# Slot attention in a twelve-stage kernel: score buffers released by PSUM bank, one merged query and key weight, gate terms put into PSUM, reset gate first

## The reference, cut to what matters

```python
Pn = rmsnorm(P, input_norm_w)
k_proj = Pn @ Wk.T;  v_proj = Pn @ Wv.T
for _ in range(3):
    q = rmsnorm(slots, slot_norm_w) @ Wq.T
    attn = softmax(q @ k_proj.T * 256 ** -0.5, axis=slots)
    attn = attn / (attn.sum(over context) + 1e-6)
    slots = gru_cell(attn @ v_proj, slots, wi, wh, bi, bh)
# gru_cell: r = sigmoid(ir + hr); z = sigmoid(iz + hz)
#           n = tanh(inn + r * hn); return (1 - z) * n + z * h
```

## Time and profile before

| | us |
|---|---|
| median of three runs | 1587.63 |
| the profiled execution | 1585.95 |
| its span in the trace | 1583.7 |
| first round, first score to last attend (14.40 to 107.61) | 93.2 |
| tail and head between rounds one and two (107.88 to 125.70) | 17.8 |

### The profile page before, as it was taken

The page is one execution under the profiler, slowest core; times in us unless marked ns, Lnnn a source line. Parts: engine busy times, 40 slices in busy tenths (PEclk is TensorE's granted clock), DMA queues, the critical chain, the costliest instruction groups (busy, mean ns, idle before and its releaser), DMA issues. The chain is left out here.

```text
span 1583.7 us, 29660 instructions
## 1 busy us (share of the span) xinstructions
PE 1460.7 (92%) x11444; PEld 1106.4 (70%) x11444; DVE 926.7 (59%) x2822; ACT 764.3 (48%) x1787; POOL 82.0 (5%) x74
## 2 busy tenths in 40 slices
PE   7998999987999888899999999999999798889987
PEld 6977979955767654467777777777776696656765
DVE  5654545547466442377777777777777275444434
ACT  5744535523122131266676666676766681323222
POOL 2310000000000000200000000000000000000000
PEclk9999999988999999899999999999999998989999
DMA  9946414310156379511100001111100300507760
GB/s 330 325 141 238 161 48 163 117 40 8 61 225 233 131 282 344 221 36 37 37 32 21 24 35 36 37 36 37 36 2 2 124 2 1 228 1 241 271 258 4
DMA packets 66011, 182.28 MB, mean 115 GB/s; under 512 B 5201, under 2 KB 47185, under 8 KB 64465
## 3 DMA queue, kind: packets, MB, share of 16 engines
q1 hardware_dynamic: 65152, 171.98, 30.2%
q10 hardware_dynamic: 720, 8.42, 1.3%
HBM read 179.86 MB, written 0.52 MB: 114 GB/s over the span
## 5 line engine op out<-in xcount | busy, mean ns | idle before, releaser
L1978 ACT ACTIVATE cross_s<-cross_s,cross_shift 128x896 f32<-128x896 f32 x224 | 215.2, 1031 | 39.2 <-DVE cross_shift L2062 39.2
L1972 ACT COPY cross_eT<-cross_ring 128x512 f32<-128x512 f32 x280 | 153.1, 591 | 143.3 <-PE cross_ring L1900 143.3
L1900 PEld LDWEIGHTS cross_ring<-consts,cross_s 128*128 128x128 f32 x1568 | 168.3, 141 | 56.3 <-issue 44.2
L1900 PE MATMUL cross_ring<-consts,cross_s 128*128 128x128 f32 x1568 | 197.0, 277 | 6.1 <-ACT cross_s L1978 6.1
L2053 DVE CUSTOM_DVE_ANT_0 cross_s<-cross_scores,cross_mask,cross_top 128x448 f32<-128x448 f32 x224 | 141.3, 681 | 84.5 <-PE cross_scores L1892 84.5
L436 ACT ACTIVATE slots_probs<-slots_scores,slots_bias,ctx_rinv 128x128 f32<-128x128 f32 x294 | 130.0, 460 | 109.7 <-DVE slots_bias L484 109.7
L2053 DVE CUSTOM_DVE_ANT_0 cross_s<-cross_scores,cross_mask,cross_half_max 128x448 f32<-128x448 f32 x224 | 141.4, 682 | 13.4 <-PE cross_scores L1892 13.3
L155 PE MATMUL slots_scores<-slots_qkT,slots_ctxT 128*128 128x128 f32 x1176 | 139.9, 277 | 9.1 <-DMA slots_ctxT<-in_ctxT 8.3
L155 PEld LDWEIGHTS slots_scores<-slots_qkT,slots_ctxT 128*128 128x128 f32 x1176 | 138.4, 194 | 13.1 <-DMA slots_ctxT<-in_ctxT 9.3
L386 PE MATMUL slots_attended<-ctx_rows,slots_probs 128*128 128x257 f32 x588 | 135.2, 380 | 1.2 <-DVE slots_pooled L498 1.1
L1892 PE MATMUL cross_scores<-cross_keysT,cross_qz 32*128 32x448 f32 x896 | 121.8, 589 | 4.3 <-DVE cross_half_max L2053 3.1
(11 more groups left out here) (794 smaller groups left out, 2141.2 us busy)
## 6 DMA issues: line engine op xcount, KB each, us to landing
slots_ctxT<-in_ctxT SPq DMA_DIRECT2D x42, 896.0 KB, 4.7
ctx_rows<-in_ctx_rows SPq DMA_DIRECT2D x28, 896.0 KB, 7.3
ctx_rows<-in_moe_w SPq DMA_DIRECT2D x24, 1024.0 KB, 9.7
cross_ctxT<-in_ctxT SPq DMA_DIRECT2D x13, 896.0 KB, 4.5
padded_ctxT<-in_ctxT SPq DMA_DIRECT2D x12, 896.0 KB, 4.6
plain_ctxT<-in_ctxT SPq DMA_DIRECT2D x12, 896.0 KB, 4.7
local_layers<-in_w_local SPq DMA_DIRECT2D x2, 4552.0 KB, 14.5
weights_region<-in_moe_w SPq DMA_DIRECT2D x8, 1024.0 KB, 10.9
```

The lines of the kernel that those rows point to most:

```text
L1900: last = pe.transpose(bank(("turn", u, t))[:, j * P:(j + 1) * P], s_buf[:, u % 2, j, t * P:(t + 1) * P], K.ident)
L1972: act.copy(eT[:, u % 2, t], bank(item)).then_inc(st("emptied_act"), 1)
L1978: act.activation(rows, rows, ACT.Exp, bias=shift[:, u % 2, j:j + 1], scale=SCALE).then_inc(st("exp"), 1)
```

## The change

1. **By bank.** `score`, the `ctxT` loads, `maxima` and `exponentials` are each cut into a part of four tiles and one of three (`BANK_TILES`), with semaphores and loads for each.
2. **Order of the first round.** Mean squares run one group ahead, ScalarE's between the two parts of the exponentials, VectorE's behind `normalise`. The loads of rows are sent by a table, `ROWS_AT`.
3. **One weight.** Wq and Wk are multiplied once on TensorE and scaled by both norm weights (`qk_weight`). A head is then one product of two matmuls from `slotsT`, a scaling by 1/rms, two transposes and a copy. The slots themselves are transposed, so the norm runs beside.
4. **Pooling.** The division by the sum is put into the transposition: `pooled` times a diagonal matrix `diag`. The input norm weight goes into Wv once.
5. **Gates.** Biases are put into PSUM by a product with the identity, the old slots' part is accumulated on them at moments given in the code, and ScalarE reads the gates from PSUM. Reset comes first, then the candidate, then update.
6. **TensorE's idle products** go from the heads; six stand behind the last round. The loads of the next stages' weights on ScalarE's queue are sent behind the square root instead of ahead of it.

```diff
-ROWS_AHEAD = 2
 ROWS_SENT = 4
+ROWS_AT = {1: [1], 2: [2], 3: [3, 4], 4: [5, 6], **{n: [n + 2] for n in range(5, GROUPS - 2)}}
+BANK_TILES = (range(0, 4), range(4, TILE))
...
+                    for s, part in enumerate(BANK_TILES):
+                        if n >= 2:
+                            sp.wait_ge(st("scored"), 2 * (n - 2) + s + 1)
+                        keys = slice(part[0] * P, part[-1] * P + P)
+                        sp.dma_start(ctxT[:, b, :, keys], T["ctxT"][g:g + 1, :, :, keys].rearrange("o p c m -> p (o c) m")).then_inc(st(f"ctxT_in{b}{s}"), 16)
...
-                    pe.wait_ge(st(f"ctxT_in{b}"), (n // 2) * 16 + 16)
-                    if n >= 2:
-                        pe.wait_ge(st("exp"), n - 1)
-                    for t in range(TILE):
-                        last = product(pe, sc[b][:, t], [(ctxT[:, b, c, t * P:(t + 1) * P], qkT[:, c]) for c in range(DC)])
-                    last.then_inc(st("scored"), 1)
...
                 K.weights.wait(pe, "slots")
+                fold_qk(0)
                 for it in range(SLOT_ITERS):
-                    idle_products(pe, K, scores[:, 1024:1536], 10 if it else 4)
+                    pe.wait_ge(st("slots_ready"), it + 1)
...
+                    if it == 0:
+                        fold_qk(1)
+                        pe.wait_ge(st("qk_weight"), DC)
+                    pe.wait_ge(st("slotsT"), it + 1)
+                    product(pe, qk_mm, [(slotsT[:, k], qk_weight[:, k]) for k in range(DC)]).then_inc(st("qk_mm"), 1)
+                    pe.wait_ge(st("qk"), it + 1)
+                    transposes(pe, qkT_mm, qk, K.ident, DC).then_inc(st("qkT_mm"), 1)
+                    if it:
+                        reset_slots()
...
+                    if it == 0:
+                        K.weights.wait(pe, "gates")
+                        pe.wait_ge(st("gate_rows"), 1)
+                        reset_hcand_rows()
+                    else:
+                        update_rows()
+                        update_slots(0)
                     pe.wait_ge(st("pooled"), it + 1)
-                    transposes(pe, pooledT_mm, pooled, K.ident, DC).then_inc(st("pooledT_mm"), 1)
+                    for c in range(DC):
+                        last = pe.matmul(pooledT_mm[:, c], pooled[:, c * P:(c + 1) * P], diag[:, :], start=True, stop=True)
+                    last.then_inc(st("pooledT_mm"), 1)
+                    if it == 0:
+                        reset_slots()
+                    else:
+                        update_slots(1)
                     pe.wait_ge(st("pooledT"), it + 1)
                     for c in range(DC):
                         last = product(pe, updT_mm[:, c], [(wv[:, k, c * P:(c + 1) * P], pooledT[:, k]) for k in range(DC)])
                     last.then_inc(st("upd_mm"), 1)
+                    for k in range(DC):
+                        pe.matmul(hcand_mm, slotsT[:, k], wh[:, k, 2 * D:], start=False, stop=False)
+                    if it == 0:
+                        inn_rows()
                     pe.wait_ge(st("updT"), it + 1)
                     for k in range(DC):
-                        last = pe.matmul(rz, updT[:, k], wi[:, k, 0:2 * D], start=False, stop=k == DC - 1)
-                    last.then_inc(st("rz_mm"), 1)
-                    product(pe, inn, [(updT[:, k], wi[:, k, 2 * D:]) for k in range(DC)]).then_inc(st("gates_mm"), 1)
+                        last = pe.matmul(reset, updT[:, k], wi[:, k, 0:D], start=False, stop=k == DC - 1)
+                    last.then_inc(st("reset_mm"), 1)
+                    for k in range(DC):
+                        last = pe.matmul(inn, updT[:, k], wi[:, k, 2 * D:], start=False, stop=k == DC - 1)
+                    last.then_inc(st("inn_mm"), 1)
+                    if it == 0:
+                        update_rows()
+                        update_slots(0)
+                        update_slots(1)
+                    for k in range(DC):
+                        last = pe.matmul(update, updT[:, k], wi[:, k, D:2 * D], start=False, stop=k == DC - 1)
+                    last.then_inc(st("update_mm"), 1)
+                    if it + 1 < SLOT_ITERS:
+                        pe.wait_ge(st("hcand"), it + 1)
+                        reset_hcand_rows()
+                        pe.wait_ge(st("cand_in"), it + 1)
+                        inn_rows()
+                    else:
+                        idle_products(pe, K, scores[:, 1536:2048], 6)
...
+                    g, b, a = n % GROUPS, n % 2, n % HELD
+                    for s, part in enumerate(BANK_TILES):
+                        act.wait_ge(st("bias"), 2 * n + s + 1)
+                        for t in part:
+                            last = act.activation(probs[:, a, t], sc[b][:, t], ACT.Exp, bias=bias[:, a, t:t + 1],
+                                                  scale=K.rinv[:, g * TILE + t:g * TILE + t + 1], accum_out=total[:, a, t:t + 1])
+                        last.then_inc(st("exp"), 1)
+                        if s == 0 and n + 1 < GROUPS:
+                            squares(n + 1)

...
+                    act.wait_ge(st("reset_mm"), it + 1)
+                    act.activation(gate[:, 0:D], reset, ACT.Sigmoid).then_inc(st("reset"), 1)
                     act.wait_ge(st("cand_in"), it + 1)
                     act.activation(cand[:, :], cand[:, :], ACT.Tanh).then_inc(st("cand"), 1)
+                    act.wait_ge(st("update_mm"), it + 1)
+                    act.activation(gate[:, D:2 * D], update, ACT.Sigmoid).then_inc(st("update"), 1)
...
                     for g in range(GROUPS + 1 + SLOT_LAG):
                         n = it * GROUPS + g
                         if g < GROUPS:
                             maxima(n)
-                        if it == 0 and g + ROWS_AHEAD < GROUPS:
-                            squares(g + ROWS_AHEAD)
                         if 1 <= g <= GROUPS:
                             normalise(n - 1)
+                        if it == 0 and g + 1 < GROUPS:
+                            squares(g + 1)
+                        if it == 0 and g == GROUPS:
+                            K.weights.wait(dve, "gates")
+                            link(dve.tensor_tensor(W["bi"][:, D:2 * D], W["bi"][:, D:2 * D], W["bh"][:, D:2 * D], ALU.add))
+                            dve.tensor_tensor(W["bh"][:, D:2 * D], W["bi"][:, 0:D], W["bh"][:, 0:D], ALU.add)
+                            for k in range(DC):
+                                last = dve.tensor_scalar(wv[:, k], wv[:, k], W["in_w"][:, k:k + 1], None, ALU.mult)
+                            last.then_inc(st("gate_rows"), 1)
```

More of the change, by code:

```diff
@@ L315, in stage_slots @@
         at = [attended[:, b * 512:b * 512 + D + 1] for b in range(2)]
-        slotsT_mm, normedT_mm = two(attended[:, 0:D]), two(mm[:, 0:D])
-        qT_mm, qkT_mm = two(mm[:, 512:512 + D]), two(mm[:, 512 + D:1024])
+        slotsT_mm, qk_mm = two(attended[:, 0:D]), attended[:, 512:512 + D]
+        qkT_mm = two(attended[:, 0:D])
+        qk_weight_mm = [mm[:, c * 512:c * 512 + D] for c in range(DC)]
         pooledT_mm, updT_mm = two(scores[:, 0:D]), two(scores[:, 512:512 + D])
-        rz, hn, inn = mm[:, 0:512], mm[:, 512:768], mm[:, 768:1024]
+        reset_hcand, reset, hcand_mm, inn = mm[:, 0:2 * D], mm[:, 0:D], mm[:, D:2 * D], mm[:, 512:512 + D]
+        update = scores[:, 1024:1024 + D]
         def tiles(g):
@@ L387, in attend, with fold_qk, reset_hcand_rows, inn_rows @@
                     last.then_inc(st("attended"), 1)
+                def fold_qk(c):
+                    product(pe, qk_weight_mm[c], [(wq[:, k, c * P:(c + 1) * P], wk[:, k]) for k in range(DC)]).then_inc(st("qk_weight_mm"), 1)
+                def reset_hcand_rows():
+                    pe.matmul(reset_hcand, K.ident, W["bh"][:, D:3 * D], start=True, stop=False)
+                def inn_rows():
+                    pe.matmul(inn, K.ident, W["bi"][:, 2 * D:], start=True, stop=False)
+                def update_rows():
+                    pe.matmul(update, K.ident, W["bi"][:, D:2 * D], start=True, stop=False)
@@ L389, in _, with reset_slots, update_slots @@
+                def reset_slots():
+                    for k in range(DC):
+                        pe.matmul(reset, slotsT[:, k], wh[:, k, 0:D], start=False, stop=False)
+                def update_slots(k):
+                    pe.matmul(update, slotsT[:, k], wh[:, k, D:2 * D], start=False, stop=False)
                 K.weights.wait(pe, "slots")
+                fold_qk(0)
                 for it in range(SLOT_ITERS):
-                    idle_products(pe, K, scores[:, 1024:1536], 10 if it else 4)
@@ L430, in _ @@
                 norm_scalar(act, st, "ln", lnb)
-                def exponentials(n):
-                    g, b, a = n % GROUPS, n % 2, n % HELD
-                    act.wait_ge(st("bias"), n + 1)
-                    for t in range(TILE):
-                        last = act.activation(probs[:, a, t], sc[b][:, t], ACT.Exp, bias=bias[:, a, t:t + 1],
```

(12 more changed lines are left out.)

139 lines of the change are left out of this document (57 added, 82 removed).

## The result

The changed kernel takes 1572.78 us (median of five runs, 1570.65 to 1576.36) against 1587.63 for the kernel before: ratio 0.9899, 95% interval 0.9883 to 0.9915. That is 14.85 us faster, where 28 to 30 were forecast. The profiled execution is 1572.78 us with a span of 1570.5, so in the profiles the gain is 13.2.

What follows compares the result with a forecast made beforehand. TensorE was taken to bound the group loops, a serial chain the stretches between. Gains in loops, heads, tails and next stage summed to 28.4 us, giving 1557.5 from the profile, 1559.2 from the median; forecast 1558, range 1551 to 1571.

Steps and rivals of the forecast that it cites:

- no wait in round three and 0.5 us in round two: Start of the group loops: predicted waits of the third scores for `ctxT`; rounds two and three gain 3.8 and 2.85 us.
- its bounds are 0 and 3.1: Third scores of round two: limits set on the 0.5 us wait, 3.1 us being the wait before the change.
- The ring is under the 6.17 of TensorE, so after the start it catches up: Round one's loop: the dependency cycle through bias, exponentials, squares and `rinv` takes 5.7 us a group, below TensorE's 6.17.
- Halving the packets of `ctxT` I take at nothing: `ctxT` loads in the group loops: smaller packets were claimed to cost 0, with 350 GB/s when busy either way.
- the next stage: Start of the stage after the rounds: six idle products keep the clock up, 3 us gained, bounds -0.6 and 3.4.
- Later stages only shift: Everything after the next stage's start: claimed to move earlier in time without gaining or losing any.
- heads: Start of rounds two and three, slots to first score: 3.9 us instead of 6.2, each gaining 2.3 us.
- the other tails: Rounds two and three, last `add` to new slots: 8.1 us instead of 11.6, a gain of 3.5 us.
- A: Rival, round one: GpSimd's step meets the 1.09 us product, a ring turn takes 6.8 us; 8 us lost, 1566; chance 0.11.
- B: Rival: starts still wait, round two 3.1 us, round one loses the clock, next stage gains nothing; 1566; chance 0.12.
- C: Rival: TensorE's clock falls at the tails' starts and in heads; 34 us given back, 1591.5; chance 0.05.
- D: Rival: unseen limits leave half of each chain term and nothing in the loop, about 1578 to 1583; chance 0.04.

Runs made afterwards that it cites:

- Experiment 3: The kernel before, with the two loads of the next stage's weights sent behind round two's square root instead of ahead of it; 1592.78 us, ratio 1.0007.
- 4: The changed kernel, with both loads of the next stage's weights sent in round one's tail, ahead of ScalarE's wait for `reset_mm`; 1566.77 us, ratio 0.9857.
- 12: The changed kernel, with both loads of the next stage's weights sent behind the reset sigmoid of round one; 1568.52 us (one run).
- 9: The kernel before, with both weight loads sent early, ahead of the wait for round one's gates; 1586.81 us, ratio 0.9982.
- Experiment 11: The changed kernel with weight loads sent in round one's tail, each `ctxT` load from the third group on bringing only one of two chunks; 1565.32 us (one run).
- 2: The changed kernel, with each half of `ctxT` contiguous in DRAM and SBUF, in pieces of 4096 and 3072 bytes per partition; 1576.09 us, ratio 0.9907.
- 6: The changed kernel, with weight loads sent in round one's tail and contiguous `ctxT` halves in packets of 4 and 3 KB; 1565.43 us, ratio 0.9846.
- Experiment 8: The changed kernel, with weight loads sent in round one's tail and without the six idle products behind the last gate product; 1563.92 us (one run).
- experiment 10: The changed kernel, with weight loads in round one's tail, contiguous `ctxT` halves and `add(n-3)` ahead of the squares on VectorE; 1565.17 us, ratio 0.9846.

## Why the prediction was wrong, step by step

The direction was right and the time 14.8 us too low. The step that failed is "no wait in round three and 0.5 us in round two", in its second half, with "its bounds are 0 and 3.1". The wait measured 7.41 us and its slowed scores cost 1.5 more: 8.4 us beyond the forecast, of the 8.7 by which that loop missed it. I had most of the numbers for it. The DMA list gives 4100, 768 and 896 KB (the first two were not among my rows), the rows about 350 GB/s when the DMA is busy, and the send time moves against the first score from 8.0 us ahead to 3.3. The wait before was no upper bound: what hid the load was the head and its lead, and the change shortened both by 4.7 us in all. The sum 3.10 + 4.7 = 7.8 could be made from the rows, and the wait measured 7.41. Experiment 3 shows the send time alone (2.29 later, 2.68 more wait), 4 and 12 show it taken back (waits of 0.34 and 2.32), and 9 shows that the kernel before had little to gain from it.

The second step is in "The ring is under the 6.17 of TensorE, so after the start it catches up", a loop of round one in which only the start and 0.1 us at the end are held up and the DMA costs nothing. Loop 1 gained 2.1 us instead of 4.65. Its DMA share rose to 0.90 from 0.83. Its waits for `ctxT` and `add` behind attend 0 add up to 1.8 us, and from start to start they cost 2.6: the steps are 3.82 and 3.70 us long where 3.05 is normal (`ctxT`), 3.85 where 3.12 is, and the last one about 0.4 too long (`add`). That is about the miss of 2.55. Experiment 11 brings the round to its forecast by removing half of the bytes and packets of `ctxT`. "Halving the packets of `ctxT` I take at nothing" misreads the edit, since they fall to a quarter, from 7168 to 2048 and 1536 bytes; what that costs round one no run settles (experiments 2 and 6 disagree).

The third, smaller, is the next stage: 2.0 us for 3, within its bounds. Experiment 8 puts the idle products at 2.4. The sum of the terms is 28.45. With 8.7 us missed in loop 2, 2.55 in loop 1, 1.0 in the next stage, 0.4 in all other terms and the 2.7 lost later ("Later stages only shift", which these two executions do not bear out), the 13.2 us of the profiles are left.

What held: the first score at 13.09 (forecast 13.45), attend 0 at 24.23 after 1.28 us of idle time (25.0 and 1.6), heads of 3.97 us from the slots' end (3.9), 10.05 from the last `add` to slots in round one (10.0), 3.25 for 3.5 in the other tails, round three 2.74 for 2.85, and the first two rows of the next stage at 1.97 and 2.83 us (1.8 and 2.7).

The rivals: A did not occur. The biases of the first groups, on VectorE's timeline, stand 5.66 to 6.05 us apart, where 5.7 was forecast, and the product (L545) ends at 24.18, before GpSimd's step begins at 26.06, which takes 0.21:

```profile
21.88 0.20 DVE L535 SCALAR_TENSOR_TENSOR slots_bias<-slots_top,ctx_rinv 128x4 f32<-128x4 f32 x1 [2.65 <-POOL ctx_rinv L363]
...
23.09 1.09 DVE L545 TENSOR_TENSOR slots_probs<-slots_probs,slots_weight 128x896 f32<-128x896 f32 x1
...
27.93 0.19 DVE L535 SCALAR_TENSOR_TENSOR slots_bias<-slots_top,ctx_rinv 128x4 f32<-128x4 f32 x1 [1.93 <-POOL ctx_rinv L363]
...
33.59 0.19 DVE L535 SCALAR_TENSOR_TENSOR slots_bias<-slots_top,ctx_rinv 128x4 f32<-128x4 f32 x1 [1.72 <-POOL ctx_rinv L363]
```

The Trainium skill's exclusion of VectorE and GpSimd on a shared port (SBUF — State Buffer, Who interferes with whom) could not show here, since the product ended before GpSimd's step began. B came nearest, in its place, though not in its size or its parts: a start that waits, in round two alone, with a wait of 7.41 us where I gave it 3.1, while the next stage kept its gain. Even its 1566 is 7 us too low, and its part in round one's start did not occur: the third scores there did not wait and kept their pace. C did not occur in the changed kernel's tails or heads, whose records run at full clock; what clock was lost there was lost in the wait for `ctxT`. It can occur: in experiment 10 one head did lose the clock (0.51), with gaps no longer than elsewhere, and cost 1.9 us. The Trainium skill (TensorE: Matmul & The Clock Gate, A second HAM failure mode) tells of such swings from short gaps between groups of matmuls; that row agrees, and most executions here show none. D is excluded by the table, where the terms of the chain are there in full.

The fourth and sixth experiments are faster than both kernels (0.9857 and 0.9846, where the changed kernel has 0.9899); the simplest edit that pays is to send the weights when ScalarE has issued round one's exponentials. Left open: why the clock falls in some heads and starts and not in others, what the smaller packets cost round one, and whether the 2.7 us that are gone by the end recur.

## What to carry to other kernels

When a chain is shortened, look at every load that is sent during it and stands ahead of a transfer wanted after it: its hiding time shrinks by the same amount. Add up the bytes from the send to the first transfer that is waited for and divide by the rate of a full DMA; in the five traces here where the DMA stayed full, the end of the wait followed the send time, and not the work that was made faster. And do not count on slack in a stretch with a DMA share of 0.83: here round one waited for DMA as soon as its engines were faster.

## What the runs showed of the hardware

- 5.9 MB on two queues took 17.1 (the changed kernel and experiment 12), 17.6 (before) and 17.8 us (experiment 3) from the first issue to the start of the work that needs the last, and 16.0 in experiment 2: 332 to 369 GB/s. With what else was on its way, the engines moved 369 to 381 GB/s in all five.
- After an idle time of 2.32 us (experiment 12) TensorE fell to 1.2 GHz for a part of the next windows of 4 us (means of 0.72 and 0.85), after 2.50 us (experiment 8) it was at 0.50, that is 1.2 GHz; after 3.10 us it stayed at 1.00, 2.4 GHz. The length of the gap alone does not tell.
- The first 84 score records of round one took 9.84 to 9.87 us in three executions (the changed kernel, experiments 4 and 6) and 11.2 to 11.4 in three others (2, 10 and 11). In experiment 2 the granted clock was 0.50 from 13.8 to 17.0; in 10 and 11 the profile gives 1.00 there although single records last up to 583 ns, so it does not say why. Such a start costs 1.3 to 1.6 us; nothing in the edits explains in which execution it comes.
